# One-hots of the counting stage: two operations over a whole batch in place of four over halves

## The reference, cut to what matters

```
s = Wx[v_tgt] @ a_w[h, :d] + Wx[v_src] @ a_w[h, d:] + a_b[h]
s = leaky_relu(s, 0.2);  alpha = segment_softmax(s, v_tgt, n)
outs.append(segment_sum(alpha[:, None] * Wx[v_src], v_tgt))      # 8 heads
...
out = segment_sum(norm[:, None] * h[row], col)                   # the convolution
```

## Time and profile before

| | |
|---|---|
| median of 3 runs | 568.38 us (567.61 to 569.0) |
| the profiled execution | 568.89 us, span 567.1 us |
| VectorE busy | 473.7 us (84%) |
| TensorE busy | 501.0 us (88%) |
| ScalarE busy | 342.2 us (60%) |
| one-hots (L940) | 100 instructions, 92.1 us, from 16.8 to 144.8 us |
| counting matmuls (L1445) | 552 instructions, 72.1 us |
| merges (L1452) | 2 groups of 92 instructions (into C, into C2), 28.0 and 27.8 us |

### The profile page before, as it was taken

The page is one execution under the profiler, slowest core; times in us unless marked ns, Lnnn a source line. Parts: engine busy times, 40 slices in busy tenths (PEclk is TensorE's granted clock), DMA queues, the critical chain, the costliest instruction groups (busy, mean ns, idle before and its releaser), DMA issues.

```text
span 567.1 us, 12112 instructions
## 1 busy us (share of the span) xinstructions
PE 501.0 (88%) x4629; PEld 371.2 (65%) x4630; DVE 473.7 (84%) x933; ACT 342.2 (60%) x662; POOL 72.8 (13%) x83
## 2 busy tenths in 40 slices
PE   1879999887589999999899899989899998899995
PEld 1767777666488888888677544544466696566652
DVE  7999999799899999995898748995877786967681
ACT  5365555567889999994675523344435548756730
POOL 3000000000000000000000020123243410222342
PEclk9989999999899999999999979999999999999999
DMA  7970000002001111100000077000001129675111
GB/s 179 359 273 2 1 2 1 2 10 88 3 39 57 49 49 48 49 3 1 1 1 2 0 253 285 1 1 1 3 21 58 57 65 371 233 248 205 60 52 51
DMA packets 25306, 45.14 MB, mean 80 GB/s; under 512 B 6961, under 2 KB 7205, under 8 KB 25248
## 3 DMA queue, kind: packets, MB, share of 16 engines
q1 hardware_dynamic: 23264, 39.16, 20.2%
q0 software_dynamic: 1952, 5.18, 2.5%
q10 hardware_dynamic: 32, 0.01, 0.0%
HBM read 33.23 MB, written 11.95 MB: 80 GB/s over the span
## 4 chain that ended last, share of the span: by engine, by line
PE 48%; DVE 34%; issue 8%; DMA 4%; ACT 3%; POOL 1%; ACTq 0%; POOLq 0%; DVEq 0%
PE bank L1378 7%; PE bank L1643 5%; PE bank L1767 5%; PE bank L1402 5%; PE bank L1445 4%; DVE work L1072 4%; DVE big L940 4%; PE bank L1452 4%; PE bank L1356 3%; PE bank L1549 3%; PE bank L1562 2%; PE bank L1738 2%; DMA aux<-xperm_scratch 2%; DMA out<-aux 2%; DVE rings L1072 2%
## 5 line engine op out<-in xcount | busy, mean ns | idle before, releaser
L940 DVE TENSOR_TENSOR big<-mid 128x1536 f16<-128x1536 f16 (+1 forms) x100 | 92.1, 980 | 0.4 <-PE bank L1452 0.4
L1445 PE MATMUL bank<-big 128*128 128x160 f16 x552 | 72.1, 248 | 4.4 <-DVE big L940 4.4
L1549 PE MATMUL bank<-big,work 128*128 128x130 f16 x1080 | 67.4, 224 | 8.4 <-DVE work L1072 8.4
L1549 PEld LDWEIGHTS bank<-big,work 128*128 128x128 f16 x1080 | 64.3, 100 | 10.4 <-DVE work L1072 4.9
L1445 PEld LDWEIGHTS bank<-big 128*128 128x128 f16 x552 | 51.7, 111 | 7.0 <-DVE big L940 6.5
L656 ACT ACTIVATE mid<-aux,small 128x1280 f16<-128x1280 f32 x36 | 47.3, 1349 | 0.7 <-DVE work L1072 0.4
L1562 PE MATMUL bank<-big,mid 128*128 128x260 f16 x400 | 47.1, 275 | 0.1
L1643 PE MATMUL bank<-mid 128*128 128x512 f16 x200 | 47.2, 379 | 0.0
L555 ACT ACTIVATE big<-bank 128x160 f32 x92 | 27.9, 303 | 26.7 <-PE bank L1452 25.3
L555 ACT ACTIVATE mid<-bank 128x160 f32 x92 | 27.7, 302 | 25.6 <-PE bank L1452 24.2
L1562 PEld LDWEIGHTS bank<-big,mid 128*128 128x128 f16 x400 | 38.2, 96 | 7.5 <-issue 0.3
(11 more groups left out here) (310 smaller groups left out, 1122.1 us busy)
## 6 DMA issues: line engine op xcount, KB each, us to landing
big<-in_L_ffn_W SPq DMA_DIRECT2D x10, 1024.0 KB, 11.0
mid<-in_L_ffn_W SPq DMA_DIRECT2D x6, 1024.0 KB, 13.0
xperm_scratch<-work SPq DMA_DIRECT2D x1, 5753.0 KB, 20.3
aux<-thr_scratch SPq DMA_DIRECT2D x8, 640.0 KB, 3.7
aux<-xperm_scratch SPq DMA_DIRECT2D x8, 523.0 KB, 4.0
row<-in_x SPq DMA_DIRECT2D x1, 2304.0 KB
aux<-in_L_gnn_Ws SPq DMA_DIRECT2D x4, 256.0 KB, 4.5
work<-in_L_gnn_W SPq DMA_DIRECT2D x1, 1024.0 KB, 13.8
```

The lines of the kernel that those rows point to most:

```text
L940: return V.tensor_tensor(out.rearrange("p c (v two) -> p c v two", two=2), values.rearrange("p (v two) -> p v two", two=2).unsqueeze(1).to ...
L1445: mm(count_bank(base, k)[:, 0:RW], L_ring[:, slot, k * CH + j, :], R_ring[:, slot, k * CH + j, :], start=j == 0, stop=False)
L1549: ins = mm(acc_region(h, t), weighted[i % NC][:, t * P:(t + 1) * P], VP[:, s, part, h, :, :].rearrange("p b f -> p (b f)"), start=False, s ...
```

## The change

The middle batches (b = 1 to 21) are no longer made in two halves, each with a left and a right operation. One operation makes all 24 left one-hots, one makes all 24 right ones. The wait for the slot now asks for all eight pairs of batch b - 2 ahead of the first operation, and `onehots` goes up by eight at once behind the second. In batches 5 to 14 the evacuation of a tile, which stood between the halves, stands between left and right. Batches 0 and 22 are as they were.

```diff
-            def half_onehots(b, half):
-                n = LC // 2
-                c = slice(half * n, (half + 1) * n)
-                e = slice(b * LC + half * n, b * LC + (half + 1) * n)
-                at_least(v, "counted", (b - 2) * LB + (half + 1) * (LB // 2))
-                onehot(L_ring[:, b % 2, c, :], iota_lo, loT[:, e, :], n, P)
-                onehot(R_ring[:, b % 2, c, :], iota_q, qT[:, e, :], n, RW).then_inc(sem("onehots"), LB // 2)
+            def left_onehots(b):
+                at_least(v, "counted", (b - 1) * LB)
+                onehot(L_ring[:, b % 2, :, :], iota_lo, loT[:, b * LC:(b + 1) * LC, :], LC, P)
+
+            def right_onehots(b):
+                onehot(R_ring[:, b % 2, :, :], iota_q, qT[:, b * LC:(b + 1) * LC, :], LC, RW).then_inc(sem("onehots"), LB)
...
                 elif b:
-                    half_onehots(b, 0)
+                    left_onehots(b)
                     if b - 4 in BEGIN:
                         evac_a(BEGIN[b - 4])
                         if BEGIN[b - 4] == T - 1:
                             scores()
-                    half_onehots(b, 1)
+                    right_onehots(b)
```

## The result

| | before | after |
|---|---|---|
| median, 17 runs each | 569.0 us | 572.72 us |
| ratio of the two (95% interval) | | 1.0062 (1.0040 to 1.0084), +3.5 us (2.3 to 4.8) |
| profiled execution, its span | 568.89, 567.1 us | 570.75, 568.9 us |
| TensorE, VectorE busy | 501.0, 473.7 us | 499.6, 472.1 us |
| one-hots (L940) | 100, 92.1 us | 58, 89.4 us |

The kernel became slower, as forecast, by more than the 2.4 us forecast (which lies at the lower end of the interval). The ratio leaves out executions more than 1.5% above the fastest of their kernel, such as the changed one's 581.7 us. The median of 572.72 us lies in the range, near its upper end of 572.9, and the kernel before stood at 569.0 here, 0.6 above the 568.4 that the forecast starts from.

The account below looks back on a forecast made before the run. TensorE was taken to bound the tile batches, VectorE from 104.74 us, TensorE and ScalarE from 130 us. Start term 0.92 plus late term 1.5 made +2.4 us on 568.4: 570.8 us, range 569.0 to 572.9.

Parts of the forecast that it names:

- The price of an operation: VectorE's one-hots: 0.52 ns an element plus 0.07 us per operation, so a whole batch takes 3.73 us, not 3.88.
- The start term: Batch 2's left one-hots wait for merge (0,7), making TensorE's first linear matmul 0.92 us later, carried to batch 13.
- my sign of being wrong: First linear matmul not later, VectorE's batches no shorter than 3.88 us, or one-hots in the chain after batch 19.
- The tile batches: Batches 3 to 12: TensorE sets the pace at 6.37 us a batch, so the new wait and hand-over cost 0.
- the cover: Tile batches: merge (5,7) ends 1.07 us before VectorE starts batch 7; some 0.5 us left after the change.
- The late term: From batch 14: whole-batch hand-over makes count (19,0) start 1.5 us later, and TensorE and ScalarE carry it on.
- just no wait: Batch 19: merge (17,7) is over at 128.7 us, just when VectorE is ready, so VectorE does not wait.
- both terms at half: Lower end of the range, 569.0 us: start and late terms at half, a little below the late term alone.
- The clock: Rival, chance 0.12: TensorE's waits from batch 14 bring one more half-clock spell among the last batches, 1.5 us more, 572.3 us.
- VectorE to the end: Rival, chance 0.08: VectorE sets the pace through batches 14 to 22, so removed instructions pay: 565.5 us, or 567.1.

Follow-up runs that it names:

- two profiles with equal starts: The changed kernel against one with halves up to batch 13 and whole batches 14 to 21; the latter measured 1.0058 of before.
- the filled and the open wait: Both: halves up to batch 13, whole 14 to 21; open 1.0058 of before, filled with 13 matmuls of zeros in TensorE's wait before batch 14, 1.0047.
- the comparison that gave 5.2 us (1.0092): The changed kernel run again, unaltered, against the kernel before on the same chip: 1.0092 (1.0061 to 1.0123; six executions).
- right split: Changed kernel with right one-hots in two operations, the first handing over half the batch: 1.0008 (0.9984 to 1.0032) of before.

## Why the prediction was right, point by point

- *The price of an operation.* About 1.75 and 2.15 us forecast, 1752 and 2150 ns measured. A batch steps on 3.75 us (115.89 to 119.64), where 3.73 was taken.
- *The start term.* 0.92 us forecast, 0.92 measured from the release of the slot to the first linear matmul, and 0.99 between two profiles with equal starts. By the times as they stand, my sign of being wrong came true, as the first linear matmul is at 41.01 and not later than 41.23; only the distance shows the term, since batch 2 could go on 1.14 us earlier in this execution. What I missed is that it hangs on the clock: with a start at half clock TensorE sets that stretch and the term is gone. By time it was never resolved.
- *The tile batches.* Cost 0, forecast and measured (63.51 us in both kernels), and the cover did go: VectorE waits 0.6 to 1.3 us in three late ones. TensorE has the end there.
- *The late term.* 1.5 us forecast, 1.9 measured without a fall. Two terms were short. Batch 14 took 2.00 us from (14,4) to (14,7) (112.12 to 114.12), not the 1.82 read off a batch in which TensorE had waited right ahead of (14,4), so ScalarE was late by 0.51 us and not 0.4; and batch 19's "just no wait" for (17,7) was a wait, since (17,7) starts at 128.54 and ends at 128.84, and VectorE is ready at 125.00 + 3.75 = 128.75. The mechanism was as described: batch 19 handed over as a whole, and from there TensorE and ScalarE. (The lower end of the range was called both terms at half, which would be 569.6 and not 569.0.) The new waits of VectorE for batches 21 and 22 cost nothing.
- *The clock.* I gave it 0.12 as a rival and argued against it from the old wait of 1 us. That step failed, and the rival's 3.9 us (572.3) lie nearer to the measured 3.5 than my 2.4. It also rests on a wrong reading: the old trace has more than one spell at half clock. Behind the last merge TensorE stands still for 4.59 us, and the clock falls there (TensorE in order of time; the stretch behind with busy times, granted clock and DMA):

```profile
153.15 3.08 PE L1549 MATMUL bank<-big,work 128*128 128x130 f16 x27 [4.59 <-DVE work L1072]
```

```profile
151.80:158.50 6.70, 5.35 (x50) 5.38 (x51) 6.70 (x9) 4.79 (x4) 0.00 (x0) 0.50 0.00 0
```

Of the seven profiles with a wait of 1.56 to 2.7 us ahead of batch 14, five have a fall at it; of the seven without such a wait (five) or with it filled (two), none has. A fall costs 0.8 us between the two profiles of the changed kernel (44.95 and 45.79) and 1.2 us between the filled and the open wait (45.06 and 46.23). That makes 0.92 + 1.88 + 5/7 x (0.8 to 1.2) = 3.4 to 3.7 us. That this meets the 3.5 of the runs is in part luck: the start term is absent where the start is at half clock, and 5/7 is a share over several kernels. In the comparison that gave 5.2 us (1.0092), the profile accounts for 2.7 (43.07 to 45.79). The mean granted clock of five of its six executions was 0.971, against 0.977 of the kernel before on that chip, about twice what one fall of 3.4 us takes off (my estimate: 3.4 x 0.5 / 570 = 0.003); where the rest lies isn't shown. The profiled pair of the result had no fall, and it differs by 1.86 us because the start term is hidden by an earlier first count.
- *VectorE to the end.* The saved time did go from VectorE's one-hots (92.1 to 89.4 us, 2.7 of the 2.9 forecast) and reached the end nowhere: in the tile batches they became waits, in batches 14 to 19 they were set against the hand-over, later they became waits for slots. The rule on grouping of the Trainium skill ("Perfetto Trace Analysis", "Optimizing Scalar/DVE Operations") has the size right; its condition, a saturated engine, did not hold where the end was set.

That the clock falls because of the gap is strongly suggested by its absence when filled (two profiles) or when there is no gap (five), and its presence in five of seven. By time it was not shown. Why the clock stays up in the other two stays open. The Trainium skill, "TensorE: Matmul & The Clock Gate", Part 1, says that the clock is held down by default and that activity releases it; falls behind waits, and none with the wait filled, agree.

## What to carry to other kernels

In this kernel, merging two operations of a producer would have saved their fixed cost only where that engine sets the end, and it delayed the consumer's first piece by half a batch wherever the consumer was about to be the bound; look for that place (here a table load some batches before the end) before looking at busy shares. If something is to be merged, keep the last operation ahead of a hand-over split: with one left operation and two right halves the time could not be told from that of four operations. A one-off wait on TensorE, here of 1.56 to 2.7 us, can cost a second time through its clock, and useless matmuls in it are a cheap test for that.

## What the runs showed of the hardware that I had not expected

- The granted clock fell to half at a single wait of 1.56 us (right split) and of 2.6 us, after more than 60 us at full speed, and not behind one of 1 us; the same kernel does it in some executions and not in others. While it lasts, a pair takes 0.67 us instead of 0.35.
- The length of the wait alone does not decide. Behind the counting stage all 14 profiles have a fall at the wait of 4.59 us and at one of 1.87 us (324.56 us in the old trace), five have one at a wait of 2.93 us (481.6 us there), and none has one at a wait of 1.65 us (270.73) or 1.52 us (381.27). What tells these apart was not tested.
- At the start the clock is at half for 3.4 us in some executions and for 10 to 17 us in others (five stretches of 5 us, from 20 us on, at 0.82, 0.50, 0.50, 0.50 and 0.97 in the second profile of the changed kernel). In the two profiles of the changed kernel the first linear matmul comes 20.1 and 23.8 us behind the first count: a difference as large as the change under study.
- The cost of a one-hot operation is a straight line from 768 to 3840 elements: 0.52 ns an element and about 0.15 us, of which 0.07 show in the step to the next.
